# First attention stage: the sine and cosine products are added on GpSimd, and TensorE sums four terms a chunk

## What is computed

```python
z = x @ W_in                                   # keys, decay logits, and the complex query q
z_mem = causal_conv(z[..., :160], taps=4)
k_val = z_mem[..., :128].reshape(b, l, 32, 4)
p_w = exp(clip(score_scale * z_mem[..., -32:], -20, 20) + log_tw)
phi = k_val[..., None] * theta                 # 8 angles for each of 32*4 features
den = cumsum(p_w)
num_re = cumsum(p_w * cos(phi)); num_im = cumsum(p_w * sin(phi))      # over positions
s_re = num_re / den; s_im = num_im / den
out_re = sum(s_re * qr + s_im * qi, axis=-1)   # over the 8 angles
out_im = sum(s_im * qr - s_re * qi, axis=-1)
y = silu(out_re * norm_re * diag(W_re) + out_im * norm_im * diag(W_im))
return y @ W_out
```

## Time and profile before

| | us |
|---|---|
| median of 3 runs | 1645.52 |
| lowest and highest run | 1644.72, 1647.11 |
| the profiled execution's own time | 1646.25 |
| its span in the trace | 1644.5 |
| PE busy, in the span | 1242.8 |
| POOL busy, in the span | 407.6 |
| the first attention's laps, 34 to 265 us of the span | 231.0 |

### The profile page before, as it was taken

How to read it: one execution, slowest core, us unless ns; L and a number is a source line. 1 busy time by engine, 2 the same in 40 slices (tenths; PEclk the granted TensorE clock), 3 DMA queues, 4 the chain that set the end, 5 groups by cost and what they waited for, 6 DMA issues and landing times.

```text
span 1644.5 us, 27787 instructions
## 1 busy us (share of the span) xinstructions
PE 1242.8 (76%) x9126; PEld 867.8 (53%) x9126; DVE 1078.2 (66%) x3103; ACT 748.9 (46%) x1175; POOL 407.6 (25%) x626
## 2 busy tenths in 40 slices
PE   4989988999958777655678766677676999967776
PEld 2656657888833333354344435566563444446665
DVE  5564664666666777345788876677765666656777
ACT  3333342233316666553677653343331566533332
POOL 4344441000023232111545512122212222100000
PEclk8988989999978999887888986888876999978998
DMA  7000000000000000000000000000000000000000
GB/s 297 1 1 0 1 1 1 0 0 0 0 1 1 1 0 1 1 0 0 1 2 0 1 1 1 0 0 1 0 1 0 2 1 0 2 1 0 0 0 26
DMA packets 5683, 14.30 MB, mean 9 GB/s; under 512 B 224, under 2 KB 4448, under 8 KB 5088
## 3 DMA queue, kind: packets, MB, share of 16 engines
q1 hardware_dynamic: 5600, 13.26, 2.1%
HBM read 12.21 MB, written 1.05 MB: 8 GB/s over the span
## 4 chain that ended last, share of the span: by engine, by line
issue 46%; PE 26%; DVE 12%; POOL 5%; ACT 4%; DVEq 3%; POOLq 2%; DMA 1%; ACTq 0%; SPq 0%
PE PS L892 3%; PE PS L1046 2%; PE PS L994 2%; PE PS L988 2%; PE PS L971 2%; PE PS L909 2%; POOL trs L378 2%; PE PS L891 1%; PE PS L1216 1%; PE PS L876 1%; PE PS L1358 1%; DVE w_l0f L1854 1%; POOLq L377 1%; DVE mx L1744 1%; PE PS L1368 1%
## 5 line engine op out<-in xcount | busy, mean ns | idle before, releaser
L1744 DVE TENSOR_REDUCE mx<-PS 128x2 f32<-128x512 f32 (+1 forms) x256 | 155.4, 620 | 81.5 <-PE PS L994 72.3
L638 ACT ACTIVATE w_l0f<-PS 128x512 f32<-128x512 f32 (+1 forms) x256 | 137.3, 543 | 102.2 <-PE PS L1001 99.8
L376 POOL TENSOR_TENSOR tve<-tmv,eps 128x2 f32<-128x2 f32 x64 | 12.6, 197 | 590.9 <-DVE tmv L1528 589.7
L797 ACT ACTIVATE sg<-PS 128x512 f32<-128x512 f32 (+1 forms) x104 | 60.3, 580 | 201.4 <-PE PS L1439 201.3
L1439 PE MATMUL PS<-hT_padded,w_l0f 128*128 128x256 f32 x512 | 122.3, 385 | 0.0
L837 PE MATMUL PS<-w_const,h 128*128 128x128 f32 x128 | 32.4, 342 | 104.7 <-DVE h L1519 95.2
L2151 DVE TENSOR_TENSOR y<-sg,PS 128x512 f32<-128x512 f32 (+1 forms) x104 | 69.2, 666 | 59.4 <-ACT sg L797 47.0
L1439 PEld LDWEIGHTS PS<-hT_padded,w_l0f 128*128 128x128 f32 x512 | 94.8, 194 | 11.0
L837 PEld LDWEIGHTS PS<-w_const,h 128*128 128x128 f32 x128 | 16.2, 164 | 130.5 <-DVE h L1519 86.2
L1368 PE MATMUL PS<-w_l2f,y 128*128 128x128 f32 x512 | 77.0, 300 | 9.2 <-ACT y L755 6.5
L1368 PEld LDWEIGHTS PS<-w_l2f,y 128*128 128x128 f32 x512 | 74.8, 215 | 16.4 <-ACT y L755 9.4
(11 more groups left out here) (381 smaller groups left out, 3272.6 us busy)
## 6 DMA issues: line engine op xcount, KB each, us to landing
w_l0f<-in_l0f SPq DMA_DIRECT2D x1, 3076.0 KB, 13.9
w_l2f<-in_l2f SPq DMA_DIRECT2D x1, 2214.0 KB, 19.9
w_l3f<-in_l3f SPq DMA_DIRECT2D x1, 1736.0 KB, 23.5
w_l0a<-in_l0a SPq DMA_DIRECT2D x1, 1392.0 KB, 7.8
result<-X SPq DMA_DIRECT2D x1, 896.0 KB, 4.6
X<-in_x SPq DMA_DIRECT2D x1, 768.0 KB, 10.0
w_l1f<-in_l1f SPq DMA_DIRECT2D x1, 582.0 KB, 15.6
PT<-in_cbf SPq DMA_DIRECT2D x1, 576.0 KB, 10.9
```

Source lines behind the costliest of these rows:

```text
L638: act.activation(P8[:, hh % 8, 0:width], PS[:, hh % 2, 0:width], ACT.Exp, scale=SM_SCALE).then_inc(a["pt"], 1)
L797: act.activation(sg[:, c % 2, 0:cols], gate, func).then_inc(f["sg"], 1)
L1744: dve.tensor_reduce(mx[:, hh, 0:nm], PS[:, 2 + hh % 2, 0:nm * keys].rearrange("p (t k) -> p t k", t=nm), AX.X, ALU.max).then_inc(a["mx"], 1)
```

## The change

POOL gets an addition for each chunk: it waits for both products of the chunk and adds the sine part to the cosine part in place, a 128x512 fp32 instruction. `sums(u, c)` on PE now waits for that addition (`a_add`) and not for the products (`a_pr`), and takes 4 matmuls of 128 columns, not 8. POOL's order is written anew: the weights of the next unit's chunk 0 go ahead of the addition of this unit's chunk 3, and the addition of chunk 0 stands ahead of `tail_rstd`. DVE's and ACT's order is as it was.

```diff
+                    def weigh(u, c):
+                        pool.wait_ge(a_trig, u * CHUNKS + (c + 1))
+                        if c == 0:
+                            pool.wait_ge(a_p, u + 1)
+                        for b in (cb, sbuf):
+                            ins = pool.tensor_tensor(by_angle(b[:, c]), by_angle(b[:, c]),
+                                                     over_angles(pws[u % 2][:, c // 2]), ALU.mult)
+                        ins.then_inc(a_pp, 1)
+
+                    def add_parts(u, c):
+                        pool.wait_ge(a_pr, u * CHUNKS + (c + 1))
+                        pool.tensor_tensor(product(c, 0), product(c, 0), product(c, 1), ALU.add).then_inc(a_add, 1)
+
+                    weigh(0, 0)
                     for i in range(NB):
-                        pw = pws[i % 2]
-                        for c in range(CHUNKS):
...
-                            if c == 0:
-                                head_rstd(i + (head0[l] + 2))
-                            if c == 1 and i:
-                                tail_rstd(i + tail0[l])
+                        head_rstd(i + (head0[l] + 2))
+                        weigh(i, 1)
+                        add_parts(i, 0)
+                        if i:
+                            tail_rstd(i + tail0[l])
+                        weigh(i, 2)
+                        add_parts(i, 1)
+                        weigh(i, 3)
+                        add_parts(i, 2)
+                        if i < NB - 1:
+                            weigh(i + 1, 0)
+                        add_parts(i, 3)
                     tail_rstd(NB + tail0[l])
...
                     def sums(u, c):
-                        pe.wait_ge(a_pr, u * CHUNKS + (c + 1))
+                        pe.wait_ge(a_add, u * CHUNKS + (c + 1))
                         if c == 2:
                             pe.wait_ge(hd_hT, u + (head0[l] + 2))
-                        for g in range(2):
-                            of = by_angle(product(c, g))
-                            for m in range(HALF_M):
-                                ins = pe.matmul(PS[:, 6 + c // 2, L:L + P], ident, of[:, :, m, :],
-                                                start=c % 2 + g + m == 0, stop=c % 2 + g + m == 2 + HALF_M - 1)
+                        of = by_angle(product(c, 0))
+                        for m in range(HALF_M):
+                            ins = pe.matmul(PS[:, 6 + c // 2, L:L + P], ident, of[:, :, m, :],
+                                            start=c % 2 + m == 0, stop=c % 2 + m == HALF_M)
                         ins.then_inc(a_sum, 1)
```

More of the change, by code:

```diff
@@ L234, in block_program @@
         y_ready, x_done = sem("y_ready"), sem("x_done")
-        a_w, a_soft, a_z, a_lg, a_p, a_red, a_trig, a_pp, a_cum, a_pr, a_sum, a_arg, a_sil, a_ty, a_yT = (
-            sem("a_" + n) for n in "w soft z lg p red trig pp cum pr sum arg sil ty yT".split())
+        a_w, a_soft, a_z, a_lg, a_p, a_red, a_trig, a_pp, a_cum, a_pr, a_add, a_sum, a_arg, a_sil, a_ty, a_yT = (
+            sem("a_" + n) for n in "w soft z lg p red trig pp cum pr add sum arg sil ty yT".split())
         AT = {l: {n: sem(f"t{l}_{n}") for n in (own + " qkv tr m st pt pv ot otr o oT oTs").split()}
@@ L508, in _ @@
                 if l == L0_ATTN:
-                    for i in range(NB):
-                        pw = pws[i % 2]
-                        for c in range(CHUNKS):
-                            pool.wait_ge(a_trig, i * CHUNKS + (c + 1))
-                            if c == 0:
[L514 to L519, removed]
-                                head_rstd(i + (head0[l] + 2))
-                            if c == 1 and i:
-                                tail_rstd(i + tail0[l])
+                    def weigh(u, c):
[10 more added lines that the diff above has]
+                    weigh(0, 0)
+                    for i in range(NB):
+                        head_rstd(i + (head0[l] + 2))
[10 more added lines that the diff above has]
+                        add_parts(i, 3)
                     tail_rstd(NB + tail0[l])
```

## The result

The changed kernel takes 1664.02 us in the median of 4 runs (1661.77 to 1664.57); the kernel before takes 1645.12 beside it (1642.26 to 1647.11). The ratio is 1.0114, with a 95% interval of 1.0096 to 1.0131: 18.9 us slower. The forecast was 1644, within 1639 to 1651.5, so it was wrong, and on the side to which 0.27 had been given. The profiled execution took 1664.57, with a span of 1662.0.

The account below looks back on a forecast made before the run. The prediction took a periodic chain of six laps, 29.80 us each, as the bound, with PE busiest. Laps of 29.7 gave -0.6 and the ends -1.1, sum -1.7: from the median 1645.52 to 1643.8, said as 1644, range 1639 to 1651.5.

Parts of the forecast that it names:

- Six laps on the path: The block's chain repeats from cumulate(u, 1) to the next unit's; six times 29.80 us before, 29.7 forecast.
- a chunk's saving of 0.89 us at 2.4 GHz: Sums on PE: four fewer matmuls of 128 columns per chunk save 0.89 us, or 1.8 at 1.2 GHz.
- only sums(u, 0) and sums(u, 1) counting: Sums of chunks 2 and 3 lie beside other work, so only those of chunks 0 and 1 are on the path.
- The addition of chunk 3 turns part 2 into a chain over the weights (u + 1, 0): Sums(u, 3) waits for POOL's addition behind the next unit's weights; PE idles 4.5 us and most likely loses its clock.
- Part 2 at 17.1: End of cumulate(u, 2) to cumulate(u + 1, 1): 15.67 us before, 16.2 forecast at 2.4 GHz, 17.1 at 1.2 GHz, taken.
- The addition at 1.24: POOL's 128x512 addition per chunk takes 1.24 to 1.25 us, like the product with the weights; ends 0.77 and 1.72.
- Part 1 at 12.1 to 13.2: Cumulate(u, 1) to the end of cumulate(u, 2): 12.1 us with the clock back by the denominators, 13.2 with the clocks of before.
- the 0.3 allowed for: At the denominators, a later X from unit u - 1 costs -0.2 to 0.4 us more; 0.3 taken.
- The clock comes back early: Rival, chance 0.29: PE's burst restores 2.4 GHz by the denominators in nearly every lap; 29.2 us a lap, so 1641.
- stays down: Rival, chance 0.27: PE at 1.2 GHz through denominators, sums and convolve; lap 31.3 us, so 1653.5 in all laps.
- The ends, forecast -1.1: Outside the six laps: +0.5 us in the first lap, -1.6 behind 240.37 in unit 7.
- The rival on the shared port: POOL additions and DVE instructions contend for SBUF: up to 6 us for six laps, 1650; inside the ranges, no chance of its own.

Follow-up runs that it names:

- half_sums: The kernel before with the sine part left out of the sums, 4 matmuls a chunk and no addition anywhere: 1630.62 us, ratio 0.9917.
- Add3_first: The changed kernel with POOL's addition of chunk 3 ahead of the weights of the next unit's chunk 0: 1653.29 us, ratio 1.0052.
- La_psum: The changed kernel with exponents clamping in place in PSUM, so its 64-column addition `la` has one operand from SBUF, not two: 1657.33 us, ratio 1.0084.
- Tail_first: The changed kernel with tail_rstd ahead of POOL's addition of chunk 0 and nothing else: 1657.23 us, ratio 1.0072.
- adds01: The changed kernel with POOL additions for chunks 0 and 1 alone; sums of chunks 2 and 3 take eight terms again: 1643.74 us, ratio 1.0001.
- adds01_tail: The changed kernel with POOL additions for chunks 0 and 1 alone, and tail_rstd ahead of the addition of chunk 0: 1634.03 us, ratio 0.9926.
- Warm_pe: The changed kernel with six extra unused matmuls of 512 columns on PE ahead of the wait of sums(u, 3): 1660.67 us, ratio 1.0110.
- adds01_dve: The kernel before with additions for chunks 0 and 1 alone, on DVE right behind the products, GpSimd as before: 1658.86 us, ratio 1.0098.

## Why the prediction was wrong, point by point

- **Six laps on the path, a chunk's saving of 0.89 us at 2.4 GHz, only sums(u, 0) and sums(u, 1) counting**: right for sums(u, 0), and the matmuls alone gave 13.5 us (half_sums). Of the saving on sums(u, 1) only 0.3 us reached the end of part 2 there, because turns(u + 1, 1) came to lie beside POOL's products; the prediction had set it at nothing for another reason, the wait for the addition (u, 3).
- **The addition of chunk 3 turns part 2 into a chain over the weights (u + 1, 0)**: right in kind. PE idles 6.1 us, sums(u, 3) is at 1.2 GHz, and DVE's arguments(u) waits for PE, as named. Add3_first gives 2.5 us of part 2 back.
- **Part 2 at 17.1**: the step that failed. It measured 18.8. The sum held that "those weights do not move against the end of cumulate(u, 2), since products(u, 2), exponents and turns(u + 1, 0) on DVE and trig on ACT are untouched". They are untouched in the program and not in time: POOL's addition (u, 2) is released by products(u, 2), at the instant in which DVE goes on to exponents. From the end of cumulate(4, 2) to the end of the weights it is 183.49 - 173.94 = 9.55 us and not 8.45. Of this 1.1, `la` is 1.0, and a product stretched from 1.26 to 1.44 the rest. La_psum takes the 1.0 back.
- **The addition at 1.24**: mis-sized at the one place where it counts. It is 1.26 us alone and 1.70 behind L1666, for 0.45 in part 2; its upper end in the prediction had been 1.72, held for unlikely from the median of 31 products, but what decides is whether a DVE instruction is beside it. With 0.1 more in sums(u, 3) the three make the 1.7 us between 17.1 and 18.8, 10 us in six laps.
- **Part 1 at 12.1 to 13.2**: 13.4 in the chain's count, just outside. X was later than the 0.3 allowed for: at high clock PE waits 2.15 us for it. Part 1 was forecast at 12.1 with the clock back early; in the four laps with the high clock and the wait it was 13.6, 12.5, 14.2 and 14.2 (the timeline's count), because in three of them convolve ran partly at 1.2 GHz behind the wait. Against the middle taken for the forecast, 12.6, part 1 costs some 5 us in six laps. Tail_first, and adds01 against adds01_tail, show that the place of tail_rstd is worth 7 to 10 us in all, as much as the place of the addition (u, 3).
- **The clock comes back early or stays down**: neither came as it was drawn. In the changed kernel part 1 goes between 12.5 and 14.2, where before it went between 12.5 and 15.5, so the clock did not stay down more than it had. It did fall anew in three laps, behind the wait for X, for 1.2 to 1.7 us each. Warm_pe, which kept it up in sums(u, 3), moved the median by 3.3 us, which is not clear of noise.
- **The ends, forecast -1.1**: the first lap was +2.75 and the last stretch +1.85, a miss of 5.7 us. The first lap has the long part 2 as well, and unit 7 the low clock; how the 5.7 divides was not measured. Part 2, part 1 and the ends make 21 us on the forecast of -1.7, and the block did end 19.1 later. The prediction also said that it is wrong if anything behind 265 us changes by more than a few tenths: the seven other blocks were 1.5 us shorter together in the profiled executions, for which no cause was looked for.
- **The rival on the shared port** stood in the prediction, with "0.4 us a lap in front of trig". It was priced by the overlap of two long instructions, and the short one, `la`, was overlooked. Rows of the trace before that the prediction does not show had the price in them (27.80 and 29.19 above). "GPSIMD Engine Reference" of the Trainium skill, section 1, names the condition: a VectorE instruction in a two-port mode or with two inputs from SBUF. The traces agree with it: `la`, L1664, L1666 and L1671 were held, and instructions with an operand in PSUM were not. Section 3.1 of the same page of the Trainium skill gives 2.6 cycles an element for GpSimd, by which the addition is 1.1 us and dispatch, an estimate; the trace, with 1.26, agrees. Section 4.1 of it advises VectorE for such work; here the kernel was 25 us slower with the two additions there (adds01_dve against adds01_tail), where they met products on GpSimd.

What stays open: the split of the 24 us of waits between X, the order and the clock is not additive (add3_first 10.7, tail_first 6.8, la_psum 6.7, together only 16.5), and part 1 depends on the clock in a way that single profiles do not average out. With all three edits the kernel is still 17 us above half_sums, and most of that is not placed.

## What to carry to other kernels

Before work goes to an idle engine, look at which instructions of its neighbour will run in that very stretch, down to the short ones: an engine that releases another and goes on with its own program starts its next instruction beside the other's. An operation that takes work off an engine pays only where that work is on the path; here two of the four additions had a saving, and the other two only a price. And see what queues behind a new instruction in its engine: one microsecond in front of a small root cost a wait at the other end of the loop.

## What the runs showed of the hardware

- A DVE instruction with two operands from SBUF that is issued during a POOL elementwise instruction ends only after it, whatever its own length: 64 columns went from 0.225 to 1.22 us, 512 columns from 0.69 to 1.59 and 1.73. L1664 (one operand and scalars, 0.43 us) went to 1.30 and 1.48. POOL is held in turn, 1.26 to 1.70.
- Which of the two engines is first decides, be it by 0.09 us (tail_first: DVE 1.73 and POOL 1.27, or DVE 0.69 and POOL 1.72).
- With one of the two operands in PSUM the same `la` took 0.23 us in the middle of a POOL addition. A reciprocal of 64 columns from SBUF to SBUF (L1681) was not held either: 0.55 us beside a POOL addition, as in the trace of before, where there was none.
- A POOL addition of 128x512 fp32 takes 1.26 us, as the product with a repeated operand does.
- The kernel before itself ran from 1637 to 1651 us over three groups of runs, more than the 3 runs of the start (1644.7 to 1647.1) had shown.
